# Edge sums in four column groups, a placing product, six separately routed parts with 128-row expert tiles, and one unrolled order of stages

## What is computed

```python
xn = _layernorm(x)
x = x + _L0_gnn_ref(xn, src, dst, edge_weight, W)      # segment_sum(xn[src] * w, dst) @ W
      + _L0_mix_ref(xn[None], Wqkv, Wout, bout)[0]     # q @ (norm(k)^T norm(v)) / n @ Wout + bout
x = x + _L0_ffn_ref(_layernorm(x)[None], ...)[0]
# ffn: logits = x @ gate_w + gate_b (16 experts), the best two, softmax over the two,
#      each: relu(x @ w1[e] + b1[e]) @ w2[e] + b2[e]   (256 -> 512 -> 256)
#      y = x + weighted sum of the two; layernorm(y) * gamma + beta
```

## Time and profile before

| | us |
|---|---|
| median of three runs | 2140.08 |
| span of the profiled execution, first to last instruction | 1787.9 |
| difference, not seen by the profile | 352.2 |

### The profile page before, as it was taken

One profiled execution on the slowest core, in us unless ns is written; L12 is line 12 of the kernel. 1 busy time (PEld: TensorE's weight loads), 2 busy tenths in 40 slices (PEclk: granted clock), 3 DMA queues, 4 the chain that ended last, 5 costly groups with the idle time before them and its releaser, 6 DMA issues. The chain is left out here.

```text
span 1787.9 us, 31001 instructions
## 1 busy us (share of the span) xinstructions
PE 1375.6 (77%) x7652; PEld 1150.2 (64%) x7653; DVE 770.4 (43%) x2462; ACT 443.7 (25%) x938; POOL 1020.7 (57%) x1105
## 2 busy tenths in 40 slices
PE   0488988988988997129888888887997999999600
PEld 0366665766766886118777778776876888888500
DVE  6554544545544665303443353254401233331377
ACT  5121221222212222101111111112343444442221
POOL 2577777777776777667777776760165111130174
PEclk9999998999988998559999999998998999999855
DMA  9665456454563543247646746661687888887544
GB/s 301 179 191 186 120 186 188 118 187 143 162 199 104 157 132 104 83 150 228 216 139 222 219 127 198 220 139 32 207 283 244 253 261 258 260 274 248 155 139 125
DMA packets 178666, 327.90 MB, mean 183 GB/s; under 512 B 25360, under 2 KB 126352, under 8 KB 178448
## 3 DMA queue, kind: packets, MB, share of 16 engines
q1 hardware_dynamic: 85088, 147.69, 26.2%
q0 software_dynamic: 49728, 135.86, 26.1%
q10 hardware_dynamic: 43760, 43.26, 7.3%
HBM read 257.76 MB, written 68.94 MB: 183 GB/s over the span
## 5 line engine op out<-in xcount | busy, mean ns | idle before, releaser
L542 POOL DMA_INDIRECT ring<-normed_rows,idx x840 | 801.6, 954 | 257.1 <-issue 231.6
L1355 PE MATMUL ps<-S,ring 128*128 128x128 f32 x3360 | 465.2, 290 | 128.0 <-DMA ring<-normed_rows,idx 102.9
L1355 PEld LDWEIGHTS ps<-S,ring 128*128 128x128 f32 x3360 | 423.4, 200 | 161.0 <-DMA ring<-normed_rows,idx 114.7
L1495 PE MATMUL ps<-room 128*128 128x256 f32 x1136 | 265.4, 388 | 21.2 <-ACT room L736 14.9
L1508 PE MATMUL ps<-room 128*128 128x256 f32 x1136 | 259.7, 382 | 3.9 <-issue 3.6
L1495 PEld LDWEIGHTS ps<-room 128*128 128x128 f32 x1136 | 220.4, 195 | 56.0 <-ACT room L736 17.4
L958 DVE TENSOR_SCALAR S<-iota,dstrel,ew 128x128 f32<-128x128 f32 x840 | 237.1, 358 | 5.8 <-issue 5.4
L1508 PEld LDWEIGHTS ps<-room 128*128 128x128 f32 x1136 | 211.8, 192 | 32.7 <-issue 5.9
L969 DVE TENSOR_TENSOR aggT<-aggT,ps 128x256 f32 x210 | 88.4, 421 | 307.8 <-PE ps L1355 296.9
L1194 DVE TENSOR_TENSOR aggT<-ps,room 128x512 f32<-128x512 f32 x80 | 55.2, 691 | 357.7 <-PE ps L1508 342.2
L1373 PE MATMUL ps<-room,tT 128*128 128x512 f32 x392 | 193.9, 642 | 0.8 <-issue 0.8
(11 more groups left out here) (166 smaller groups left out, 1106.1 us busy)
## 6 DMA issues: line engine op xcount, KB each, us to landing
room<-in_w2b SPq DMA_DIRECT2D x71, 640.0 KB, 5.5
room<-in_w1b SPq DMA_DIRECT2D x71, 514.0 KB, 3.7
room<-rows_by_slot SPq DMA_DIRECT2D x80, 256.0 KB, 3.5
results_by_slot<-aggT ACTq DMA_DIRECT2D x80, 256.0 KB, 5.5
ring<-normed_rows,idx POOLq DMA_INDIRECT x840, 2.8
tile_in<-normed_rows SPq DMA_DIRECT2D x98, 128.0 KB, 2.5
rows_by_slot<-zeros ACTq DMA_DIRECT2D x7, 1664.0 KB
rows_by_slot<-zeros ACTq DMA_DIRECT2D x7, 1408.0 KB
```

What stands on the lines that cost most here:

```text
L542: pool.indirect_dma_start(out=ring[:, m % RING, :], out_offset=None, in_=table, in_offset=bass.IndirectOffsetOnAxis(ap=idx[:, half, m % HB ...
L1355: mm = pe.matmul(aggps[g % 2][:, f * W:(f + 1) * W], ring[:, m % RING, f * P:(f + 1) * P], S[:, m % RING, :], start=(t == 0 and f == 0), s ...
L1495: mm = pe.matmul(wide[s][:, f * TS:(f + 1) * TS], w1_sb[s][:, k * F + f * P:k * F + (f + 1) * P], xgT[s][:, k, :], start=(k == 0), stop=(k ...
```

## The change

The kernel is rewritten around a list of stages, `SLOTS`, made by `plan()` when the program is built. Nothing loops at run time but the general path for unsorted edges, which these inputs don't take.

**Edges.** 831 tiles (the 9 empty ones are dropped) in 70 batches of 12: four windows of three tiles. `W` is 32 targets instead of 128. The selection matrix, 128x32, is now the stationary operand and the gathered rows, 256 wide, the moving one. Window w goes to columns 32w to 32w+31 of the array (`tile_position=(0, w * W)`), and the tiles are issued so that neighbours lie in different column groups. The sums of a batch, 128 targets by 256 features, are copied by ACT (`accs`) and brought to their places and transposed by a second product with a 128x128 matrix `Pm` (`place`), and DVE adds them to `aggT`, once a batch. DVE makes the twelve selection matrices of a batch with two wide instructions. The gathered rows lie in two halves of 12 buffers; POOL waits once a batch.

**Stages.** `kv` reads the normed rows from SBUF (`X2`) instead of reloading them, over batches 0 to 19. From batch 20, `plan()` gives every batch a budget (`ROOM`, 12.8) and fills it with `mix` and `gate` (groups of up to five tiles), `moe` (one expert tile) and finishing stages. Each batch is `edges(b)`, the stages, `place(b)` on PE.

**Parts.** Six parts of 9, 9, 9, 9, 7 and 6 tiles are routed alone (`rank`, `slots`), scattered by POOL between gathers (parts 0 to 4 in batches 23, 29, 42, 55 and 65, part 5 in the end), and have expert tiles of 128 rows: 188 places. `SURE` places of each part are known to be taken and have no branch. `fresh` lets SP skip a weight load where the tile two places before had the same expert. Nine tiles of rows are finished during the gathers, the other forty in the last slot, in blocks of two groups of up to four tiles after every four expert tiles.

```diff
-GT = 4
-W = 128
-TS = 256
+GT = 3
+WIN = 4
+W = P // WIN
+BT = GT * WIN
+TS = 128
+PT = (0, 9, 18, 27, 36, 43, NT)
+KV_SLOTS = 20
+ROOM = 12.8
+PICKED_EARLY = 1
...
-                for t in range(GT):
-                    m = g * GT + t
-                    pe.wait_ge(gathered[m % RING], 16 * (h * (HB // RING) + m // RING + 1))
-                    for f in range(KD):
-                        mm = pe.matmul(aggps[g % 2][:, f * W:(f + 1) * W], ring[:, m % RING, f * P:(f + 1) * P],
-                                       S[:, m % RING, :], start=(t == 0 and f == 0), stop=(t == GT - 1),
-                                       skip_group_check=True)
+                for t in range(GT):
+                    for w in range(WIN):
+                        m = w * GT + t
+                        mm = pe.matmul(acc[b % 2][w * W:(w + 1) * W, :], S[b % 2][:, m, :], ring[:, b % 2 * BT + m, :],
+                                       start=(t == 0), stop=(t == GT - 1), skip_group_check=True,
+                                       tile_position=(0, w * W))
+                mm.then_inc(batch_done, 1)
...
+            def place(b):
+                pe.wait_ge(acc_copied, b + 1)
+                pe.wait_ge(pm_ready, b + 1)
+                for k in range(KD):
+                    mm = pe.matmul(placed[b % 2][:, k * P:(k + 1) * P], accs[b % 2][:, k * P:(k + 1) * P], Pm[b % 2][:, :],
+                                   start=True, stop=True, skip_group_check=True)
...
+                def load():
+                    e = sp.value_load(etab[0:1, g:g + 1], min_val=0, max_val=E - 1)
+                    after(sp, relu_done, g - 1)
+                    sp.dma_start(w1_sb[s], w1b[bass.ds(e, 1)].rearrange("a p w -> (a p) w")).then_inc(w1_in[s], 16)
+                    after(sp, y_done, g - 1)
+                    sp.dma_start(w2_sb[s], w2b[bass.ds(e, 1)].rearrange("a p w -> (a p) w")).then_inc(w2_in[s], 16)
...
+            def moe(p, j):
+                if j == 0:
+                    pe.wait_ge(slots_done, p + 1)
+                    xg_turn(POS0[p])
+                if j + 1 < NPOS[p]:
+                    xg_turn(POS0[p] + j + 1)
+                layer1(p, j)
+                if j:
+                    layer2(p, j - 1)
+                if j + 1 == NPOS[p]:
+                    layer2(p, j)
...
+            for b in range(NB + 1):
+                if b < NB:
+                    edges(b)
+                run({"kv": kv, "mid": mid, "mix": mix, "gate": gate, "rank": rank, "moe": moe}, b)
+                if b < NB:
+                    place(b)
```

More of the change, by code:

```diff
@@ L175, in gps_layer @@
+        fresh = sb("fresh", [1, NPOSITIONS], I32)
+        small = sb("small", [P, 144])
         flag = sb("flag", [1, 1], I32)
         idx_gen = sb("idx_gen", [P, GT], I32)
[L179 to L186, removed]
@@ L314, in gps_layer, with after @@
-        ahead = {s for group in LEADERS.values() for s in group}
-        def wait(eng, s, n):
-            eng.wait_ge(s, n + LEAD if s in ahead else n)
-        def start_counters(eng, names):
-            for s in names:
-                eng.sem_inc(s, LEAD)
-        def where_taken(eng, j, work, done, n, by=1):
-            some = eng.value_load(taken[0:1, bass.ds(j, 1)], min_val=0, max_val=1)
+        f_out = sems("f_out", 3)
+        def after(eng, s, n):
+            if n > 0:
+                eng.wait_ge(s, n)
@@ new lines, in after_turn_used, with where_taken @@
+        def after_turn_used(eng, n):
+            m = n - 2
+            while m >= 0 and TURNS[m][0] == "rank":
+                m -= 2
+            if m >= 0:
+                kind, q = TURNS[m]
+                if kind == "kv":
+                    eng.wait_ge(kv_done, q + 1)
+                elif kind == "mix":
+                    eng.wait_ge(mixed, MIX_AT[q] + 1)
+                else:
+                    eng.wait_ge(gated, GATE_AT[q] + 1)
+        def where_taken(eng, p, j, work, done):
+            g = POS0[p] + j
+            if j < SURE[p]:
+                work()
+                return
+            some = eng.value_load(taken[0:1, g:g + 1], min_val=0, max_val=1)
@@ L330, in where_taken, with run @@
             with eng.Else():
-                for s in done:
-                    if n(s) is not None:
-                        wait(eng, s, n(s))
-                    eng.sem_inc(s, by)
-        def before(j, s, each):
-            return lambda _: None if isinstance(j, int) and j < 2 else each * (j - s)
-        def prior(j):
-            return 1 if j == 0 else 2
-        def chunks(eng, first, last, body):
-            with eng.Fori(first, last) as c:
-                body(c)
-        TABLES = [(dstrel[:, :].bitcast(I32), dst), (base_i[:, :], first_dst.to_broadcast([P, NG]))]
+                eng.wait_ge(done, g)
+                eng.sem_inc(done, 1)
+        def run(stages, slot):
+            for stage in SLOTS[slot]:
+                if stage[0] in stages:
+                    stages[stage[0]](*stage[1:])
+        TABLES = [(dstrel[:, :].bitcast(I32), dst), (first_i, first_dst.to_broadcast([P, NG]))]
         CONSTS = [(ew[:, :], edge_w), (src_sb[:, :], src), (wkv_sb, wkv)]
@@ new lines, in store @@
+            def store(f):
+                for i, q in enumerate(range(*FIN[f])):
+                    sp.wait_ge(f_done, FIN_AT[q] + 1)
+                    sp.dma_start(out[q * P:(q + 1) * P, :], zt[fin_buffer(f)][:, i, :]).then_inc(f_out[fin_buffer(f)], 16)
+            finished = []
+            for b in range(NB + 1):
+                for f in finished:
+                    store(f)
+                finished = []
+                run({"mix": mix, "moe": moe, "fin2": finished.append if b < NB else store}, b)
@@ L488, in _ @@
+            for i in range(3):
+                sp.wait_ge(f_out[i], 16 * sum(FIN[f][1] - FIN[f][0] for f in FINS if fin_buffer(f) == i))
         @block.gpsimd
```

1799 lines of the change are left out of this document (791 added, 1008 removed).

## The result

The changed kernel takes 2776.03 us (median of four runs, 2770.27 to 2780.18), the kernel before 2139.72 beside it: 1.296 times as long, 95% interval 1.293 to 1.299. The forecast was 2096, the range ended at 2230. The profiled execution has a span of 2778.4 us and took 2780.18, so 1.8 us lie outside its span, not 352. Why the forecast had 352 is told with e1 and at the end of the account; it is not where the 30% are.

A forecast was written before the change was run, and what follows sets the result against it. POOL was taken to bound k and v, PE the stretch from 1400 to 1640 us. Terms 390 + 916 + 79 + 59 = 1444, plus 300 for the last slot, gave span 1744, with 352.2 outside 2096 us; range 1990 to 2230.

The forecast's parts named there:

- The step that failed: Expert tiles: first weights, issued after an earlier result, land after 3.7 us; runs of fresh tiles can't keep PE's pace.
- the DMA step: Weight traffic: four fresh tiles and 12 gathers take 24.5 us of DMA against 18.3 of PE and 15.1 of POOL.
- 70 us there: Last slot: finishing 34 tiles in six blocks delays DVE's taking of expert results, leaving 70 us exposed.
- rival B: Edge products: column groups run one after the other, 3.2 us more PE a batch, 2252 us; chance 0.13.
- k and v, 390: First stage, batches 0 to 19: runs from 57 to about 390 us, where it ended at 578 before.
- Edges, 2.0 us a batch: Narrow edge products: a batch of 12 tiles takes 2.0 us of PE, with bounds 1.3 and 5.2.
- The loop and the last slot: From batch 20 the loop ends at 1444 us; the last slot adds 300, to a span of 1744.
- Rival C, weights starve PE: Expert weights: columns pack, but DMA gives only 250 GB/s to mixed traffic, 2213 us; chance 0.20.
- An empty place, 2.9 us: Untaken expert places: 2.9 us between transposes in the earlier trace, taken as 2.3 each, 67 us for 29.
- POOL waiting for PE in the loop: Gathers in the loop: a sign expected in the changed profile, with the last gather at about 1430, not 1228.
- PE waiting for DVE in the loop: Loop from batch 20: a sign that the forecast is wrong, since only the slot computations were allowed for.
- rival D: Time outside the span: the 352.2 us aren't constant; scaled with the span, 2088 us; longer outside part, chance 0.03.

The follow-up runs named there:

- e1: The kernel before, unchanged, run once more to have its span and a trace: 2154.23 us.
- e9: The changed kernel, unchanged, at the faster level: 2422.26 us, 1.354 times the kernel before.
- e10: Changed kernel with SP requesting expert rows one tile earlier, ahead of the weights between, at the faster level: 1946.04 us, 1.088 times the kernel before.
- e11: Changed kernel with rows early, first weights two tiles ahead, small finishing steps, and ACT requesting rows from each part's third tile: 1769.95 us, ratio 0.989.
- e12: e11 with four parts instead of six (158 places, 84 fresh weights), at the faster level: 1750.61 us, ratio 0.980 to the kernel before.
- e4: Changed kernel with edge products issued three in a row in the same column group instead of alternating: 2787.2 us, one execution.
- e3: Changed kernel in its old order, most weight columns left out from each part's third place on: 2648.49 us, ratio 1.233 to the kernel before.
- e8: Changed kernel with early rows and only a small part of each weight load's columns: 1792.9 us, ratio 1.001 to the kernel before.
- e18: e12 once more, at the slower level: 2170.4 us, ratio 1.010 to the kernel before.
- e5: Changed kernel with early rows, plus SP issuing first weights two tiles ahead, before the wait for second weights: 1963.03 us, ratio 1.097.
- e13: Changed kernel with only the rows moved to ACT's queue from each part's third tile on, at the slower level: 2317.0 us, ratio 1.080.
- e15: e11 with five parts instead of six (173 places), at the slower level: 2187.63 us, ratio 1.022 to the kernel before.

## Why the prediction was wrong, by its own steps

Stages in us of the span (last edge product and first of batch 20 from the timeline). The forecast is to be read against the faster level, since its rows were of it.

| | forecast | after | e9, the same at the faster level | e10 | e11 | e12 |
|---|---|---|---|---|---|---|
| batch 20 begins | 390 | 458 | 393 | 393 | 393 | 403 |
| edges end | 1444 | 2200 | 1858 | 1552 | 1438 | 1426 |
| span | 1744 | 2778 | 2413 | 1953 | 1762 | 1748 |

*The step that failed* is "SP issues the next first weights only after the result of the tile two before has been taken". It names the wait and stops one instruction short of who stands behind it on SP: the rows of the next tile. I priced a late weight load, in the DMA step, 24.5 us per batch of four fresh tiles and 4.1 us a tile in the last slot. The rows behind that wait closed a ring through SP, DMA, PE and DVE, and in the last slot, between finishing blocks, a run of fresh tiles cost 10.2 to 12.6 us each at both levels, while three tiles in a row that kept their weights cost 3.7 each (e9, 2160.5 to 2171.7 us). The loop shows the same by the number of fresh tiles. Of e9's batches with four taken tiles, two with none fresh take 17.0 us, those with two fresh 24 to 43, with three 37 to 42, with four 45 to 47 and once 54.5. So the loop takes 1465 us against 1054 forecast; the last slot takes 555 against 300. Together 411 + 255 + 3 (k and v) = 669, which is the whole miss of the span at that level (2413 - 1744). The order edit alone takes back 460 of them (e9 to e10); the rows' own queue, the weights ahead and the small finishing steps together take another 191 (e10 to e11).

The last slot holds a second case of the same step. SP also stores the finished rows, and the next expert tile's rows stand behind that store. Six waits of PE in e9's last slot, 11.9 to 25.7 us and 117 us together, end with rows requested so. I had put 70 us there, and laid them to DVE's order of work. The longest of the six:

```profile
2149.26 1.81 SPq L562 DMA_DIRECT2D result<-ring  x4
2151.11 4.87 SPq L525 DMA_DIRECT2D room<-rows_by_slot  x3
2154.95 0.69 PE L1256 MATMUL ps<-ident,room 128*128 128x128 f32 x2 [25.66 <-DMA room<-rows_by_slot]
```

Of the cases only the sign was there: 0.36 for slower. The slowest of them, B, stood at 2252 us, and none had this mechanism.

*k and v, 390:* right, 393.

*Edges, 2.0 us a batch:* 1.43 from the first product to the next group's, near the lower bound of 1.3; the upper bound of 5.2 isn't reached even in turn, where it is 2.49 and the last product, 2.87 in all. So rival B is out: the groups run side by side. e4, where they don't, is only 11 us over the median of the changed kernel, in a kernel that waits for something else. The Trainium skill ("TensorE: Matmul & The Clock Gate", Part 3) would have the load wait unless the row group differs; here 24 loads that all fill the same 128 rows, and their 24 products, took 1.12 us from first to last start, so the measurement decides against it.

*The loop and the last slot:* with the order mended, e11 ends its loop at 1438 (forecast 1444) and its span at 1762 (forecast 1744). The nearness is partly luck: e11's batches of four fresh tiles take 21 to 24 us, not 24.5 (one, 32), and dearer waits for POOL and a last slot of 324 us, not 300, pay for that. Those waits stand where the forecast had them, ahead of the edge products of batches 24, 25, 44, 56 and 57, but they are 16.5, 10.5, 13.8, 33.9 and 11.0 us, 86 together where 59 were forecast. The 79 us by which DMA was to be longer can't be reworked from the figures given: 24 batches at 24.5 against 18.3 us would be 149, and few of them hold four fresh tiles. So the sum was a fair estimate of the work, and none of what the order of its requests would do.

*Rival C, weights starve PE:* it named DMA's rate. The changed kernel moved 138 GB/s with DMA's engines busy 39 to 53%, so no rate was the limit; e3 took 113 MB away and gained 128 of 636 us. After the order was mended, e11's weights cost 91 us in waits for landing. C's sign was right and its mechanism wrong. Nor were the first weights the longest wait, as the signs had it; the rows were.

*An empty place, 2.9 us:* the transposes of the earlier trace rows are 3.03 us apart, which over 29 places changes the sum by less than 4 us.

*DMA, 379 MB and 120 fresh tiles:* 382.84 MB and 120 loads of each kind.

*Gathers, 831 at 1.25 us:* 958 ns and 0.30 between, as in the earlier trace rows. "POOL waiting for PE in the loop" came true at 762 us, for another reason than meant.

*"PE waiting for DVE in the loop" would be wrong:* it waited for a transfer, and that transfer for DVE's taking of a result, in the fresh tiles. The sign was on the list, one link too short.

*352 us outside the span, and rival D:* wrong. The span is the time less 1.8 to 2.2 us in each profiled run; the difference was between two levels at which one kernel runs. Taken against e9, the miss is 2422 - 1746 = 676 us, against the times of the record 2776 - 2096 = 680: the wrong constant hid nothing of the cause, but a check of one number would have shown that profile and times are of different conditions.

## What to carry to other kernels

For each wait that a change puts on an in-order queue, write down the next two instructions of that queue and ask which engine needs each, and when; then follow the chain from there back to the wait. If it closes, its length is the time of one round, whatever the busy times say. Request first what is needed first, put a small load that is needed soon where no wait for something else stands ahead of it, and when one mended wait gains nothing, look in the trace at where its microseconds went before giving the theory up: two requests that block the same engine must both be moved. A rate of DMA below what other stretches of the same kernel reach says that its rate is not the limit; it doesn't say that bytes are free, as e8 gained 153 us on e10, which moved 196 GB/s.

## What the runs showed of the hardware that was not expected

**Two levels of time.** The same kernel takes 1789 us in some groups of runs and 2148 in others, every run of a group alike, and the others follow: 2422 and 2776 for the changed kernel, 1946 and 2342 for the early rows, 1748 and 2170 for four parts. The added 354 to 423 us are no constant and no factor (15 to 24%), so a ratio of one level needn't hold at the other, as e12 and e18 show. At the slower level single instructions last as long as before (the gather 951 and 954 ns) but engines are released late. Each of the nine traces of the slower level has 157 to 237 waits whose releaser is "remote" (the profile finds none near in time); none of the eleven traces of the faster level has one. The longest in the kernel after:

```profile
DVE aggT L1079 <- remote: 382.9, 24, 45.1
ACT accs L780 <- remote: 233.0, 16, 53.0
ACT room L753 <- remote: 158.2, 21, 24.9
```

Between a tile's last product and DVE's taking of it, where DVE waits, 0.04 us pass in all cases of e12 and over 1 us in 27 of 124 cases of e18, 14.9 at most. Nearly all of the difference falls while gathers run: the last edge product ends 342 us later in the changed kernel than in e9, of 366 us in all, and in the kernel before 320 us later of 364. What sets the level is open. Nothing in the kernels does, and the chip alone doesn't: the record names chip 15 for e5 to e8 at the faster level and for e13 to e15 at the slower one.

**Narrow products.** A product of 32 columns by 256 takes 0.108 us an instruction in turn and 0.049 with four column groups alternating (1.12 us over 23 steps), where the full width takes 0.216. Why the narrow one takes half in turn is open.

**The clock follows the gaps.** Where 5 us of idle time stand in each turn, the first layer's sixteen instructions take 3.1 to 3.75 us. Over such a run of 3.75 (2651.7 to 2655.1 us in the kernel after) the granted clock is 0.50, the lower of its two levels, 1.2 GHz. Where e9's tiles follow each other without a gap (2160.5 to 2171.5) it is 1.00, and they take 1.95. That is up to 1.8 us of each 10.7 us round, a second price of the same wait.
